# Second cross attention as one projection stage and eight joined turns, with its operands kept in DRAM; marks and stores of the expert loop moved

## What is computed

```python
x = x + tanh(g_xattn[0]) * L0_xattn(layernorm(x), ctx)   # 16 heads of 128, 8 key heads
x = x + tanh(g_ffn[0])   * L0_ffn(layernorm(x))          # self attention, then 16 experts, top 4
x = x + tanh(g_xattn[1]) * L1_xattn(layernorm(x), ctx)   # 16 heads of 32
x = x + tanh(g_ffn[1])   * L1_ffn(layernorm(x))          # quantized, hidden 2048
```

```python
y_dca, y_main = y[:, -16:], y[:, :-16]          # the last 16 context tokens apart
kv_dca = y_dca @ Wkv_dca + bkv_dca;  k_dca = _ln(k part);  v_dca = v part
q = _ln(x @ Wq + bq per head of 32)
k = _ln((y_main @ Wk + bk) per head);  v = y_main @ Wv + bv
ctx = softmax(q k^T / sqrt(32)) v + softmax(q k_dca^T / sqrt(32)) v_dca
return ctx @ Wo + bo
```

## Time and profile before

| what | value |
|---|---|
| median of 3 runs | 3089.94 us (3088.32 to 3096.61) |
| the profiled execution, its own time | 3089.14 us |
| its span, first to last instruction | 3087.3 us |
| TensorE matmuls busy | 2504.7 us, 81% |
| VectorE busy | 1814.6 us, 59% |
| ScalarE busy | 1530.1 us, 50% |
| GpSimd busy | 1040.6 us, 34% |
| mean granted TensorE clock | 0.917 of full |
| moved by DMA | 138 MB, mean 45 GB/s |
| second cross attention, 2173.5 to 2895.7 us | 722.2 us |

### The profile page before, as it was taken

How to read it: one execution, slowest core, us unless ns; L and a number is a source line. 1 busy time by engine, 2 the same in 40 slices (tenths; PEclk the granted TensorE clock), 3 DMA queues, 4 the chain that set the end, 5 groups by cost and what they waited for, 6 DMA issues and landing times.

```text
span 3087.3 us, 47720 instructions
## 1 busy us (share of the span) xinstructions
PE 2504.7 (81%) x15334; PEld 2075.3 (67%) x15334; DVE 1814.6 (59%) x3904; ACT 1530.1 (50%) x3064; POOL 1040.6 (34%) x1442
## 2 busy tenths in 40 slices
PE   6999999999858888888848888883578787878455
PEld 3787878787747888888727787783456565756332
DVE  2555555555546666666644444444576786867676
ACT  3444444444436666666524333330375675747544
POOL 0322222222214444444406555555133241414100
PEclk9999999999979999999958999997679798989778
DMA  2000000000010000000025444444200000020100
GB/s 76 18 18 10 17 7 17 12 15 7 1 38 18 17 17 17 17 17 17 1 64 170 150 156 149 156 149 133 60 16 9 15 1 23 1 77 1 72 7 21
DMA packets 91582, 137.98 MB, mean 45 GB/s; under 512 B 17152, under 2 KB 43776, under 8 KB 90816
## 3 DMA queue, kind: packets, MB, share of 16 engines
q1 hardware_dynamic: 84816, 114.66, 11.6%
q0 software_dynamic: 6640, 21.76, 2.1%
HBM read 119.62 MB, written 16.78 MB: 44 GB/s over the span
## 4 chain that ended last, share of the span: by engine, by line
PE 56%; issue 16%; DVE 12%; POOL 7%; ACT 6%; DMA 2%; DVEq 0%; ACTq 0%; SPq 0%; POOLq 0%
PE pair L529 6%; POOL e_w L1430 5%; PE pair L1056 5%; PE pair L557 4%; PE pair L2316 4%; PE pair L1106 4%; PE pair L492 4%; PE pair L515 3%; PE pair L2300 3%; PE pair L1128 3%; PE pair L546 2%; PE pair L1090 2%; PE pair L2326 2%; PE pair L498 2%; PE pair L488 2%
## 5 line engine op out<-in xcount | busy, mean ns | idle before, releaser
L429 ACT ACTIVATE x_p<-x_p,x_least 128x1024 f32<-128x1024 f32 x128 | 147.2, 1150 | 308.1 <-DVE x_least L385 308.1
L1753 PE MATMUL pair<-m_h,e_w 128*128 128x320 f32 x1536 | 252.6, 328 | 48.0 <-DVE e_act L1691 45.3
L1430 POOL TENSOR_TENSOR e_w<-e_raw,e_w 128x2048 fp32r<-128x2048 f32 x48 | 220.5, 4595 | 187.1 <-ACT e_w L1396 187.0
L1753 PEld LDWEIGHTS pair<-m_h,e_w 128*128 128x128 f32 x1536 | 247.2, 204 | 53.7 <-DVE e_act L1691 49.2
L369 DVE TENSOR_TENSOR x_pT<-pair,x_pT 128x512 fp32r<-128x512 f32 x256 | 164.4, 684 | 122.6 <-ACT x_pT L448 122.6
L529 PE MATMUL pair<-x_pT,x_v 128*128 128x256 f32 x1536 | 209.9, 294 | 9.2 <-DVE x_pT L369 9.2
L463 POOL TENSOR_TENSOR x_carry<-x_rtotal 128x1 f32<-128x1 f32 x128 | 24.7, 193 | 560.2 <-DVE x_rtotal L362 560.2
L529 PEld LDWEIGHTS pair<-x_pT,x_v 128*128 128x128 f32 x1536 | 194.2, 194 | 26.3 <-issue 18.3
L557 PE MATMUL pair<-x_kT,x_qT 128*128 128x512 f32 x768 | 207.5, 405 | 0.0
L968 ACT ACTIVATE s_p<-s_p,s_least 128x128 f32<-128x128 f32 (+3 forms) x256 | 143.6, 561 | 123.4 <-DVE s_least L878 123.4
L1106 PE MATMUL pair<-s_pT,s_v 128*128 128x256 f32 (+1 forms) x1152 | 159.0, 285 | 48.0 <-DVE s_pT L855 48.0
(11 more groups left out here) (321 smaller groups left out, 6226.0 us busy)
## 6 DMA issues: line engine op xcount, KB each, us to landing
e_raw<-in_L_ffn_w SPq DMA_DIRECT2D x48, 1024.0 KB, 5.4
y_rows<-hslot SPq DMA_DIRECT2D x48, 256.0 KB, 6.9
f_raw<-in_L_ffn_w SPq DMA_DIRECT2D x2, 4096.0 KB, 15.0
s_wraw<-in_L_ffn_wq SPq DMA_DIRECT2D x9, 512.0 KB, 4.5
cslot<-in_ctx SPq DMA_DIRECT2D x16, 256.0 KB, 2.8
x_wq<-in_L_xattn_Wq SPq DMA_DIRECT2D x8, 512.0 KB, 3.5
x_woraw<-in_L_xattn_Wo SPq DMA_DIRECT2D x8, 512.0 KB, 3.6
s_woraw<-in_L_ffn_wo SPq DMA_DIRECT2D x8, 512.0 KB, 3.9
```

Of the source, the lines that this page charges most:

```text
L1430: pool.tensor_tensor(dst[1][:, :, :], raw[parity][:, :, :], dst[0][:, :, :].bitcast(F32), ALU.subtract).then_inc(s_lo, 1)
L1753: mm = pe.matmul(GU[m % 2][:, j * BANK:j * BANK + CAP], w[x0][:, c, m * P:(m + 1) * P], XS[s][x1][:, c, :], start=(n == 0 and c == 0), sto ...
```

## The change

**First cross attention.** SP writes the transposed context to a DRAM tensor `ctx_stash` once, and the counts of its semaphores are handed to the second attention, which reuses them.

**Experts.** The stores move from SP to ScalarE's queue, the first two behind `tokens` of the next expert and the third behind the next expert's high part of w2. The eight marks are cut into four pairs, one behind each product. A silu of one number is put at the head of ScalarE's loop body.

```diff
-                def store(e, s):
-                    for r in range(CT):
-
-                        sp.wait_ge(s_yd, CT * (e + 1) + r + 1)
...
+                def store(e, s, r):
+                    act.wait_ge(s_yd, CT * (e + 1) + r + 1)
...
+                    act.dma_start(dst, hslot[:, k * D:(k + 1) * D]).then_inc(s_st[k], 16)
...
                     act.wait_ge(s_y, CT * (e + 1))
                     high(act, w2[0], 16 * (3 * i + (1 if s == 0 else 3)) + (0 if s else 16), s)
+                    if not first:
+                        store(e - 1, 1 - s, CT - 1)
...
                     tokens(e + 1, 1 - s)
+                    for r in range(CT - 1):
+                        store(e, s, r)
...
+                with act.Fori(1, NE // 2 - 1) as i:
+                    silu_table()
...
-                    mark(e + 2)
                     for m in range(HC):
...
                         if m >= 1:
                             part_low(m - 1)
+                        mark(e + 2, range(m * NT // HC, (m + 1) * NT // HC))
                     part_low(HC - 1)
```

```diff
+                for s in range(STEPS):
+                    u = s
+                    if u < len(units):
...
+                        add(u, "q" if name[0] == "q" else "k", kt[u % 4][:, :, :]).then_inc(s_add, 1)
...
+                    if s == B + 1:
+                        dve.wait_ge(s_wi, WI0 + 48)
+                        centre(flat(centred_weight("q")), s_cw)
...
+                    u = s - 1
+                    if 0 <= u < len(units):
+                        dve.wait_ge(s_sq, u + 1)
+                        dve.tensor_reduce(var[:, u * NH:(u + 1) * NH], sq[u % 2][:, :, :], AX.X, ALU.add).then_inc(s_var, 1)
...
+                    u = s - TLAG - 1
+                    if B <= u < len(units):
...
+                        dve.tensor_tensor(stlo[i][:, :, cols], tt[u % 2][:, :, :], sthi[i][:, :, cols].bitcast(F32),
+                                          ALU.subtract).then_inc(s_fl, 1)
```

```diff
+                    if own:
+                        pe.wait_ge(s_ld[b], 16 * 7 * (g + 1))
+                    for n in range(NU):
+                        hd, q = n // QT, n % QT
+                        if own:
+                            pe.wait_ge(s_ex, EX0 + 2 * (NU * h + n - 1))
...
+                            mm.then_inc(s_sc, 1)
+                        if own if n >= LAG else before:
+                            transposes(n - LAG)
+                        t = n - OUT_AT
+                        if before and 0 <= t < QT:
+                            project(t)
+                        if n % 2 and (own if n >= LAG + 2 else before):
+                            values((n - LAG - 2) // 2)
```

More of the change, by code:

```diff
@@ L1522, in few_sync, with body @@
             def few_sync(sp):
[L1523 to L1532 removed]
+                def body(i, s, last):
                     e = i * 2 + s
@@ L1537, in body @@
                             load(sp, 3 * s + k, e + (1 if k else 0), kind)
-                        if k == 1 and not first:
-                            store(e - 1, 1 - s)
                 sp.dma_start(count_up[:, :], a["c_count_up"].partition_broadcast(P)).then_inc(s_up, 16)
@@ new lines, in cross_attention_1, with turns, back_vector, body @@
+            OUT_AT = LAG + 2
+            assert LAG % 2 and OUT_AT + QT <= LAG + 2 + NU // 2
+            def turns(engine, body):
+                body(0, 0, "first")
+                with engine.Fori(0, NG - 1) as g:
+                    body(g, 1, "")
+                    body(g + 1, 0, "")
+                body(NG - 1, 1, "last")
+                body(NG, 0, "after")
+            def back_vector(dve):
+                dve.wait_ge(s_tb, NT)
+                def body(g, b, part):
+                    h, before, own = B * g + b, part != "first", part != "after"
@@ L2231, in gpsimd, with back_gpsimd, body @@
+                        if before and n == OUT_AT - 1:
+                            outputs(1, PAIR * h)
+                        if own and n == OUT_AT - 1 + NU // 2:
+                            outputs(0, PAIR * h + 1)
+                turns(act, body)
+            def back_gpsimd(pool):
+                def body(g, b, part):
+                    if part == "after":
+                        return
+                    h = B * g + b
+                    for n in range(NU):
                         w = n % RING
-                        pool.wait_ge(s_rt, NS * j + n + 1)
+                        pool.wait_ge(s_rt, RT0 + NU * h + n + 1)
@@ L2298, in transposes, with back_tensor, body @@
+                turns(pool, body)
+            def back_tensor(pe):
+                def body(g, b, part):
+                    h, before, own = B * g + b, part != "first", part != "after"
+                    def transposes(n):
+                        pe.wait_ge(s_pn, PN0 + 2 * (NU * h + n + 1))
+                        for i in range(2):
+                            pe.wait_ge(s_tl, TL0 + 2 * (NU * h + n - 1) + i + 1)
                             for k in range(NK // 2):
```

952 lines of the change are left out of this document (505 added, 447 removed).

## The result

| | before | after |
|---|---|---|
| median | 3089.53 us (4 runs) | 2987.51 us (4 runs, 2986.14 to 2992.28) |
| ratio, 95% interval | | 0.9668 (0.965 to 0.9686) |
| span of the profiled execution, clock | 3087.3 us, 0.917 | 2986.4 us, 0.924 |

What follows compares the result with a forecast made beforehand. Second cross attention was held bound by its rounds and serial chains at both ends of each head group, experts by TensorE with a hole; 3089.1 us less 105 (29 experts, 76 attention) gave 2984 us, range 2960 to 3015.

Steps and rivals of the forecast that it cites:

- Experts, 29: Expert stage: 64 us removed, less 22 for later output matmuls and 13 for clock loss, 29 us gained (6 to 42).
- Removed: the hole: Experts: TensorE's idle time between chunk pairs, 45.3 us, goes, with about 19 us of slow clock; together 64.
- rival 2: Experts gain nothing: last copy still waits for its store, or clock falls in 16 new holes; 3007 us, chance 0.11.
- Set-up, 49: Second cross attention: loads, VectorE's centring (12 us) and GpSimd's subtractions put the second unit's start at 49 us.
- Second unit, 3.5: Second cross attention, behind the set-up: the second unit of the pipelined stage takes 3.5 us.
- Steps, 80 + 18: Pipelined stage: 16 key/value steps at 5.0 us make 80, and late query weights add 18.
- bump: Key/value steps: VectorE waits for query weights, then centres them, 13 us; other engines' passes add 5: 18 (8 to 22).
- Query units 30: Pipelined stage: eight query units, without values, at 3.8 us each, 30 us.
- Turns, 436: Second cross attention: 128 rounds 362, projections 43, end 28, cold clock 3; 436 us (425 to 455).
- no break between turns: Second cross attention, sign in the trace after: turns follow each other without a break, next turn's loads hidden.
- Rivals 1 and 4: Pipelined stage: stores bind it, 3034 us, chance 0.17; or strided DRAM stores make the kernel slower than before, chance 0.04.
- Rival 3: Chains overlap better: steps at 4.4, bump 8, loads 11 us, no clock loss in experts; 2947 us, chance 0.08.

Runs made afterwards that it cites:

- lows_later: The changed kernel with GpSimd's passes over the weights waiting until VectorE has centred weights and biases: 2996.95 us.
- combo_a: The changed kernel with marks four and four, later waits for small constants, query weights in own memory loaded last, first score not waiting for values: 2928.6 us.
- split_marks: The changed kernel with the stores back on SP's queue, marks still two by two behind the four products: 2995.14 us.
- combo_b: combo_a with the second product's low part taken ahead of the third product and the third's behind the fourth product: 2935.2 us.
- marks_4400: The changed kernel with four marks behind the first product, four behind the second, none behind the last two: 2951.91 us.
- act_stores: The changed kernel with all eight marks back at the head of an expert, stores still on ScalarE's queue: 2971.03 us.
- combo_c2: combo_a with an expert's first W2 product taking its matmuls chunk by chunk, each behind its own low part's wait: 2916.74 us.

## Why the prediction held, point by point

The total, 2984 against 2987.5, came from the right mechanisms, but that it is so close is in part luck: errors inside the experts, the set-up and the turns cancel, the largest of them about 20 us.

- **Experts, 29 against 28.0.** The old hole went, the new one came, and half of the experts (eight of 16) lost their clock behind it, as taken, at 1.5 us each. The new hole is 2.80 us where I had 2.2, and the output matmuls start 1.83 us later than before in an expert and not 1.35, 29 us in all and not 22: I priced marks beside GpSimd at 0.65 and not the low part ahead of them at 3.16. By these rows the sum would be 64 - 29 - 12 = 23; the other 5 us are in small differences that I did not sum, such as 2.4 for chunks that now overlap by 0.16 us where the hole was. But "Removed: the hole" was put down to both edits together, and the step "Against: the copy no longer has the marks behind it" in rival 2 is wrong as a reason: with the marks left where they were, the quicker store alone gives 44.4 us of expert stretch. Given that store, the spread of the marks costs 16.7 us. I never asked what each edit gives without the other.
- **The store.** It lands after 4.6 us (forecast left it open between 6.9 and less). In SP's program it also stood behind the wait for the next weight's buffer; which of the two counts more no run separates.
- **Set-up, 49 against 46.4** (the second unit's matmuls start at 2189.08, behind 2142.67). The wait for the loads was 21.3 (22). VectorE's 12 us were 25.3, and `lows_later` shows 10.6 for them alone. It cost next to nothing here because GpSimd's six passes begin at +26.3 (27), take 20.1 us (18.5) and end at 2189.0, 0.8 us ahead of VectorE. The forecast's own terms on that path, 27 and 18.5, make 45.5: 3.5 us of its 49 have no term.
- **Second unit, 3.5 against 8.0** (2189.08 to 2197.08), the term most wrong for its size. TensorE comes out of a hole of 4.45 us, the granted clock is 0.61 in these 8.0 us, and the first 12 matmuls take 5.49 us, where I had gone by 3.02 at full clock.
- **Steps, 80 + 18 against 96.3** (2197.08 to 2293.43). Most steps with the layernorm took 5.8 us (two 6.0 and 6.5), those without 4.3 to 5.2; mean and bump (8.0 waiting, 4.8 centring) as forecast. VectorE waits there for ScalarE's z_sthi, 1.1 to 2.6 us a step, and for no store.
- **Query units 30 against 30.3, end 11 + 3.5 against about 12.7, loads 15 against 17.9** (issue at 2336.39, score at 2354.25). The values landed last, and 512 KB to 32 partitions land after 10.4 us in the median. First score at 211.6, forecast 210: set-up, steps and end came out short, the second unit and the loads long.
- **Turns, 436 against 438.5, by luck.** The two long turns hold 19.6 us over 50.5 each, which no term of the sum has: "no break between turns" holds for the loads and not for VectorE's loop. Without them the turns take 418.9, 17 less than forecast: the projections cost 5.1 us a turn over 16 rounds at 2.84 and not 6.2, the first turn is 2 us shorter than its rounds, from last score to last addition are 25.8 us (28), the round of 2.83 behind the last score was counted twice, and the 3 us for a cold clock do not show. The last four additions are 2.83 us apart where they were 1.72, as taken.
- **Rivals 1 and 4** fall: 768 KB of values in pieces of 1.5 KB landed after 3.6 us, the figure I had taken, which is 218 GB/s. The key stores, 512 KB each and two together, landed after 4.7 and 5.7 us in the median. At the 103 GB/s that the Trainium skill, "DMA: Bandwidth & Descriptors", in "Latency and other measured facts", gives for rows 4 MiB apart, two of them would have taken 10.2 us, an estimate; with planes 1 MiB apart they show no such fall. **Rival 2** was half there: the third copy still waits for its store, 2.8 and 5.2 us in turn, but TensorE waits for nothing behind it. **Rival 3** had the experts' clock wrong, and its steps of 4.4 us.

## What to carry to other kernels

When two edits cure the same wait, price each alone and each given the other: here the second one had nothing left to gain and moved work ahead of the next consumer, and cost 17 us. Before an engine's work is moved behind a product, list who waits for the moved work next; and where a short hole is left that another engine's chain sets, give the waiting engine the part of its own work that is ready: that brought 12 us where one more rearrangement of VectorE lost 7. A chain of small loads that one queue issues belongs off the first operation's wait. And where a total comes out right, check its terms by rows: here two holes of 8 us behind a loop's branch stood in a sum that fitted without them.

## What the hardware showed that I had not expected

VectorE's time for one operation depends on what GpSimd does. With both tensors in SBUF a subtraction of 512 elements takes 0.69 us alone, 4.94 beside GpSimd's passes, and 14.26 in `combo_a`, through four passes in a row; 16 elements scaled take 0.17 or 3.63. Operations with one tensor in PSUM (z_kt in `lows_later`, 0.69; e_act, 0.49) and reductions (0.67 to 0.69) kept their time beside GpSimd in the rows I read. GpSimd lost much less, 20.1 against 18.3 us. The Trainium skill, "SBUF — State Buffer", in "Who interferes with whom", states that a VectorE instruction with two SBUF inputs contends with a GpSimd instruction that reads SBUF, and that a reduction never does; the rows of the subtractions and the reductions agree. Had I used it, I would not have put VectorE's centring at 12 us; the total would have been the same, for GpSimd's passes end as late. The wait can go on over several GpSimd instructions, as the 14.26 us for 0.69 show.

TensorE's granted clock falls to the lower of its two levels (1.2 GHz of 2.4) behind short holes, and not each time: of the 14 experts between the first and the last, in seven behind 2.8 us (in 11 in `split_marks`, behind 2.8 to 2.9), five behind 1.4 us in `combo_b`, one behind 1.2 us in `marks_4400`, none behind 1.25 us in `act_stores` or 0.45 us in `combo_c2`. At 1.6 us a fall, five in 14 add 0.6 us to a hole of 1.4 us on average.
